# A loop over eight tile bodies written out as straight code, in a fused GCN, Mamba and expert kernel

## What is computed

```python
h = relu(adj @ layernorm(x) @ gcn_w + gcn_b);  h = layernorm(h) * ln_g + ln_b
xc, z = split(h @ w_in)                      # 256 + 256 channels
u = silu(causal_conv4(xc) + conv_b);  dt, B, C = projections(u)
for t in rows:                               # state: 256 channels x 16 slots
    state = exp(dt[t] * A) * state + dt[t] * B[t] * u[t];  y[t] = state @ C[t]
x1 = x + ((y + u * D) * silu(z)) @ w_out
H = gelu(layernorm(x1) @ W1 + b1);  e = argmax(H @ Wg + bg);  p = softmax(...)[e]
out = x1 + p * (H @ Wd[e] + bd[e])           # each row by its own expert e
```

## Time and profile before

| | us |
|---|---|
| three runs | 1871.58, 1872.9, 1887.38 |
| median | 1872.9 |
| the profiled execution | 1874.4 |
| its span, from first to last instruction | 1872.6 |
| DVE busy | 1548.7 (83%) |
| PE busy | 1518.5 (81%) |
| POOL busy | 875.4 (47%) |
| ACT busy | 847.2 (45%) |
| mean granted TensorE clock | 0.898 of full |

### The profile page before, as it was taken

One profiled execution on the slowest core, in us unless ns is written; L12 is line 12 of the kernel. 1 busy time (PEld: TensorE's weight loads), 2 busy tenths in 40 slices (PEclk: granted clock), 3 DMA queues, 4 the chain that ended last, 5 costly groups with the idle time before them and its releaser, 6 DMA issues. The chain is left out here.

```text
span 1872.6 us, 18473 instructions
## 1 busy us (share of the span) xinstructions
PE 1518.5 (81%) x4568; PEld 759.1 (41%) x4568; DVE 1548.7 (83%) x2049; ACT 847.2 (45%) x1500; POOL 875.4 (47%) x478
## 2 busy tenths in 40 slices
PE   6998898998989898989889898989898957245453
PEld 2443243443435453444445353545344433234342
DVE  8018999999999999998899989898899999995220
ACT  2024454545445464636354645455373636353210
POOL 0003444545454655656364646455554646475333
PEclk9999999999999999898999999998999976566777
DMA  8879999988786878787877978786878743342322
GB/s 308 283 250 392 395 391 320 358 294 290 283 298 246 314 257 298 259 305 244 292 286 272 308 258 296 259 306 229 290 248 306 258 165 138 105 144 69 96 86 50
DMA packets 165023, 479.65 MB, mean 256 GB/s; under 512 B 19989, under 2 KB 50210, under 8 KB 164914
## 3 DMA queue, kind: packets, MB, share of 16 engines
q1 hardware_dynamic: 154930, 452.19, 68.4%
q0 software_dynamic: 8832, 22.18, 3.7%
q10 hardware_dynamic: 1152, 4.19, 0.6%
HBM read 447.88 MB, written 33.75 MB: 257 GB/s over the span
## 5 line engine op out<-in xcount | busy, mean ns | idle before, releaser
L982 PE MATMUL ps_adj<-ring,nodes 128*128 128x512 f32 x2048 | 954.0, 612 | 89.3 <-DMA ring<-adj 60.7
L450 POOL TENSOR_TENSOR h_c<-hidden,bc_ring 128x1024 f32<-128x1024 f32 x256 | 602.1, 2352 | 858.4 <-DVE inject L911 735.2
L774 DVE TENSOR_TENSOR_SCAN hidden<-decay,state,inject 128x512 f32<-128x512 f32 x512 | 627.6, 1267 | 57.2 <-ACT decay L530 17.9
L982 PEld LDWEIGHTS ps_adj<-ring,nodes 128*128 128x128 f32 x2048 | 391.5, 196 | 610.2 <-issue 462.8
L530 ACT ACTIVATE decay<-dt_sb,negA 128x512 f32<-128x512 f32 x512 | 339.4, 711 | 1.0 <-DVE dt_sb L834 1.0
L911 DVE TENSOR_TENSOR inject<-dtu_sb,bc_ring 128x1024 f32<-128x1024 f32 x256 | 314.4, 1228 | 22.2 <-DMA bc_ring<-bc_dram 17.3
L858 DVE TENSOR_TENSOR y_sum<-y_sum,h_c 128x1024 f32<-128x1024 f32 x224 | 273.6, 1221 | 21.9 <-POOL h_c L450 20.6
L523 ACT COPY state<-hidden 128x2 f32<-128x2 f32 x256 | 49.3, 193 | 526.3 <-DVE hidden L774 525.6
L418 POOL DMA_INDIRECT got<-bins,row_at x72 | 93.6, 1301 | 63.5 <-DVE out_at L755 43.7
L423 POOL DMA_INDIRECT out<-o_sb,out_at x72 | 85.3, 1185 | 53.8 <-DVE dest L790 24.5
L457 POOL DMA_INDIRECT bins<-rec,dest x64 | 92.9, 1452 | 11.4 <-issue 6.0
(11 more groups left out here) (156 smaller groups left out, 1314.3 us busy)
## 6 DMA issues: line engine op xcount, KB each, us to landing
ring<-adj SPq DMA_DIRECT2D x512, 512.0 KB
bc_ring<-bc_dram SPq DMA_DIRECT2D x256, 512.0 KB, 6.3
wd_ring<-wd_rows SPq DMA_DIRECT2D x72, 320.0 KB
bins<-nodes SPq DMA_DIRECT2D x128, 129.0 KB
nodes<-x_rows ACTq DMA_DIRECT2D x8, 512.0 KB, 12.0
x_tile<-x_rows SPq DMA_DIRECT2D x16, 256.0 KB, 5.7
wd_rows<-Wd SPq DMA_DIRECT2D x8, 256.0 KB
got<-bins,row_at POOLq DMA_INDIRECT x72
```

The costliest lines, as they stand in the source:

```text
L450: nc.gpsimd.tensor_tensor(h_c[:, s % 2], hidden[:, s % 2], over_halves(bc_ring[:, s % BC_RING, 1]), ALU.mult).then_inc(hc_ready, 1)
L774: scan = nc.vector.tensor_tensor_scan(hidden[:, s % 2, h], decay[:, s % 2, h], inject[:, h], state[:, h, s:s + 1], ALU.mult, ALU.add)
L982: last = nc.tensor.matmul(ps_adj[:, 0], nodes[:, m], ring[:, g % RING, m % GROUP], start=(m == 0), stop=(m == J - 1))
```

## The change

`bodies` calls every body with a Python number, from -2 to 17, on all five engines. The hardware loop, its register, its branches and the register form of each wait value and DMA address in bodies 6 to 13 are gone from the program; `ALL`, which only the loop used, goes with them. `stages(i)` gives for i = 6 to 13 what `ALL` gave. The order of the instructions that compute or move data is the same, and so are their operands and tiles.

```diff
-        ALL = dict(adjacency=True, front=True, mamba=True, ffn=True, scatter=True, batch=True, late=True)
-
         def bodies(eng, body):
-            for i in range(-2, 6):
-                body(i, i % 2, **stages(i))
-            with eng.Fori(6, TILES - 3, 2) as i:
-                body(i, 0, **ALL)
-                body(i + 1, 1, **ALL)
-            for i in range(TILES - 2, TILES + 2):
+            for i in range(-2, TILES + 2):
                 body(i, i % 2, **stages(i))
```

## The result

| | before | after |
|---|---|---|
| median of 13 runs, us | 1872.9 | 1864.04 |
| lowest and highest | 1869.5, 1887.38 | 1852.18, 1871.37 |
| ratio, with its 95% interval | | 0.9941 (0.9918 to 0.9964) |
| span of the profiled execution | 1872.6 | 1866.9 |

The straight code is faster by 0.6%, between 0.4% and 0.8%. The medians are 8.9 us apart, and the ratio stands for 11.1 us. The forecast of 12.8 us less is a ratio of 0.9932, inside the interval.

The account below looks back on a forecast made before the run. DVE was taken to pace the kernel's middle. Terms 12.1 + 1.3 + 0.8 - 2.9 = 11.3, plus 0 to 2.9, gave 12.8 us with the middle: 1872.9 - 12.8 = 1860.1 us, 8-in-10 range 1853 to 1870.

Parts of the forecast that it names:

- part 1: DVE's three taken loop branches: gaps of 4.19, 3.57 and 4.60 us go, gaining 12.1 us.
- part 2: Branches of SP, ACT and POOL: SP's 5.6 us hole and the others' go too, priced at nothing.
- part 3: Register instructions before DVE's waits, at slot 15's inject and a body's first scan: gains of 1.3 and 0.8 us.
- part 4: DVE's waits in straight form: no overlap with the scan's end, so eight bodies lose 2.9 us.
- the main term: DVE's busy time per body, 93.35 us straight against 93.09 in the loop: 0.26 us lost per body.
- part 5: DVE's inject waits without a releaser, 2.9 us in 6 cases: gain 0 to 2.9, middle 1.45 us.
- the sum: All terms over the eight loop bodies: 11.3 to 14.2 us gained, 12.8 with the middle.
- rival C: Without SP's hole the ring is full; half of 28.3 us of waits goes, 14 more gained: 1846 us; chance 0.08.
- B: Gain goes into other waits, DVE's for decay and h_c; 10 of 12.8 us lost: 1870 us; chance 0.11.
- D: Straight code fetched too late stops DVE about 4.1 us each time; one per body gives 1893 us; chance 0.05.
- E: No change: branch is cheap, gaps belong to something else at the same places; 1872 us; chance 0.04.

Follow-up runs that it names:

- the near branches: Straight code plus a two-round loop of one register instruction before bodies 8, 10 and 12, all engines, against the kernel before: ratio 0.9931, loop stretch 794.0 us.

## Why the prediction was right, and where not

1. **The gaps of the branches** (part 1, 12.1 us). Right in place, size and cause. They are gone; one of them left gives 5 to 6 us back; DVE alone in the loop gives all of it back. The cause, code fetched again behind a far target, is shown by the near branches that cost nothing, by PE's branch, which takes 5.57 us once its loop is long enough, and by the one instruction packet inside each of the gaps when DVE alone has the loop.
2. **The other engines' holes at nothing** (part 2). Right: SP's hole alone costs nothing, and DVE alone straight has the full gain. The part names a hole of POOL too, and POOL has none: 0.28 to 0.33 us from its branch to its next instruction.
3. **Register instructions** (part 3, gain 2.1). Right: 1.5 us gone, 1.3 down to 0.4, so 2.4.
4. **Waits in the straight form** (part 4, loss 2.9). The size of the main term was right: DVE busy 746.48 against 744.70 us, 1.8 more where 2.1 was taken; the two further profiles of straight code have 747.0 and 746.8. The step that failed is the reason given for it, that a register wait lets DVE's operation overlap the scan. DVE's own form works the other way: its straight form is busy some 0.7 us less. The loss is POOL's, whose operation carries the wrong one of its waits in straight code: with POOL alone in the loop DVE is busy 743.5 us instead of 746.8, and the idle times too short for the view (the stretch less busy time and listed waits) are 15.0 us instead of 16.6. That is some 5 us in all, of which DVE's own form gives 0.7 back, so the 2.9 was too small by more than one. That it came so near with a wrong reason is luck. I had read the earlier trace rows on DVE alone; the row of `h_c` between them, which `y_sum` waits for, would have shown it.
5. **`inject` without a releaser** (part 5, 0 to 2.9, taken as half). 0.3, 2.1 and 1.2 us in the three profiles of straight code, 2.9 and 2.8 before: a gain of 1.6 on the mean, near the middle.

The pace in the eight bodies was forecast as 794 to 798 us and came out as 791.5, 792.3 and 791.5, against 809.0 and 812.6. That is 19.0 us on the means, more than the sum allows. In it are the gaps with 12.6, the register places with 2.4, `decay` with 6.9 and `inject` without a releaser with 1.6, less 2.4 for more busy time and 2.6 for more of the idle times too short to be listed (13.9 us in both profiles before, 16.3 to 16.6 after). Under half a us is left.

So the largest piece beyond the forecast is the wait for `decay`: 17.1 and 21.8 us before, 13.0, 12.8 and 12.0 after. This is what rival C describes, but its cause is not: SP alone in the loop has 12.5 us as well, with its hole. In all kernels this wait stands at one place, the scan of slot 13. One of the longest, in body 13 of the second profile of the kernel before (ACT, then DVE):

```profile
1494.86 0.69 ACT L635 ACTIVATE H<-ps_e,vec_sb 128x512 f32<-128x512 f32 x1 [7.63 <-PE ps_e L933]
1496.56 0.69 ACT L635 ACTIVATE H<-ps_e,vec_sb 128x512 f32<-128x512 f32 x1 [1.02 <-PE ps_e L933]
...
1500.75 1.32 ACT L530 ACTIVATE decay<-dt_sb,negA 128x512 f32<-128x512 f32 x2
...
1502.10 2.45 DVE L774 TENSOR_TENSOR_SCAN hidden<-decay,state,inject 128x512 f32<-128x512 f32 x2 [5.06 <-ACT decay L530]
...
1479.90:1502.10 22.20, 22.20 (x69) 12.61 (x68) 16.80 (x18) 10.61 (x19) 13.41 (x7) 0.77 0.51 174
```

`decay` is late because ACT first waits for PE's `ps_e`, and PE, busy all the time, had a mean granted clock of 0.77 in these 22.2 us, against 0.94 over the loop stretch. The same goes for the other bodies of all 14 profiles: where the trace has the clock at its lower level (1.2 GHz) for 9 us or more between the scans of slots 10 and 13, the wait is 3.6 to 5.3 us, and where it has 7 us or less, the wait is under 3.3 us. Over the loop stretch the lower level takes 99 us in both profiles of the kernel before and 75 to 85 us in the three of straight code, but 92 and 96 us in the two with POOL's waits in another order, which are straight code too and have `decay` at 19.4 and 19.8 us. So these 6.9 us go with the clock that each execution was granted, and that straight code changes this clock is not shown. What sets it stays open.

In whole runs the gain was 8.9 to 17 us by the medians and 10.7 to 15.2 by the ratios of the three times that straight code was timed; the 12.8 of the sum lie within. That the number fits so well is in part luck. In the profiles the stretches outside the loop, whose code is the same, take 1063.6 and 1066.9 us before and 1069.0 to 1075.4 after, 6.2 more on the means. They hide about what `decay` gave beyond the sum, and why they are longer no run shows.

Rivals B, D and E did not come. The fetch of straight code gave DVE none of D's stops of some 4 us: its waits with no releaser in the eight bodies are those of `inject`, 0.3, 2.1 and 1.2 us, the longest 1.1.

## What to carry to other kernels

A hardware loop costs an engine, at each taken branch, the time to fetch code that is no longer on chip, 2.2 to 5.0 us of DVE's time here. In this kernel it mattered only on the engine that sets the pace, so writing out that engine's program alone can be enough; and a loop that is still on chip, as PE's of two bodies, POOL's and the near ones here, costs nothing that can be measured. Where an operation has several waits, look in the compiled program for which of them it carries itself: it should be the one that ends last. And an edit worth 10 us can't be read from the spans of two profiles when unchanged code differs by 11; read it from the rows at its place, and time it in many runs.

## What the runs showed of the hardware

- A taken branch to a far target left DVE idle for 3.4 to 5.0 us where all engines went round together, and 2.2 to 3.6 us where it alone did. SP's next instruction came 4.6 to 5.9 us after such a branch, ACT's 4.2 to 6.0, POOL's 0.3. The same instruction to a target a few instructions back left no gap.
- In each gap of DVE alone stood one instruction packet of 8 KB, 1.3 us behind the branch, and DVE went on 1.1 to 1.3 us after the packet's end.
- PE kept a loop of two bodies on chip (branch at most 0.24 us) and fetched one of four bodies again (branch 5.57 us, PE idle for 1.94).
- A POOL operation whose last wait ends on an instruction ahead of it started 147 or 182 ns (medians) after the event, and 91 ns after it when it carried that wait itself.
- The wait of DVE for `decay` in slot 13 was 3.6 us or more only where TensorE's granted clock had been at its lower level for 9 us or more since the scan of slot 10.
